# Other slots for the third and fourth batches' stages beside the shared FFN

## The chip, the cores and the metric

The kernel runs on one core of a Trainium2 chip. The metric is the device time in microseconds (us) of one execution. Three runs of the kernel before gave 1532.86, 1532.9 and 1529.8 us; their median is 1532.86 us. A change of under 0.2%, about 3 us, can hardly be told from none.

The engines have short names in the profile: PE is TensorE (PEld its weight loads), DVE is VectorE, ACT is ScalarE, POOL is GpSimd and SP is SyncE, which only issues DMAs here. Each engine runs its own instructions in order, and waits on semaphores for the others.

## The reference

Four batches of 512 tokens with 512 features go through one pre-norm decoder layer:

```
x = x + attention(layernorm(x))        # 32 heads of 64, 8 key/value heads, rotary, causal
x = x + xattn(layernorm(x), ctx)       # einsum('emk,enk->emn', xq, wq), see below
x = x + ffn(layernorm(x))              # shared FFN on all tokens + 8 experts, top 1, 256 slots each

xq = quant_dequant_act_1x128(x)        # amax of each 128 features, scaled to 448, rounded to fp8, scaled back
wq = quant_dequant_weight_128x128(ctx) # the same with one amax for each 128x128 block
flat = where(pos < C, eidx * C + pos, E * C)   # pos: how many earlier tokens chose this expert
shared = silu(xt @ sw1) * (xt @ sw3) @ sw2     # 704 hidden features
```

So for each batch, between attention and FFN: normalise, find the peak of each group of 128, scale, round, turn (transpose), multiply with the turned and rounded context, add, normalise again, turn again, and compute the eight router logits, the choice, and each token's place in its expert.

## The kernel before, in words

All matrix products are in fp32 made of split operands: a high part (`h`) and a low part (`l`), and three matmuls for each product (`three`, L514 to L516). So every turned tile is copied out of PSUM twice: ACT writes the high part (`turn`, L1007), and then DVE subtracts it from the bank and writes the low part (`turn_lo`, L1392).

The program is one long order written out by hand for each engine. Attention takes the first 1035 us or so. Then the shared FFN goes over the tokens in eight half batches `x` = 0 to 7 (256 tokens each), then come the eight experts. Each `x` has eight steps `k`: `k` = 0 to 4 are up-projections of 24 matmuls (128x256), `k` = 5 is one of 12, `k` = 6 is the down-projection (30 matmuls of 128x512) and `k` = 7 is its last 4 matmuls, after which DVE adds the result to X (L1544). With every up-projection ACT computes the silu out of PSUM (L1054) and a high part (L1041), and DVE the product (`hm`, L1529) and a low part (`Hl`, L1516).

Beside the FFN of batch b-1 run the stages between attention and FFN of batch b; its router stages run beside its own FFN. `slots()` gives each stage of each batch a slot number, and before step `k` of half batch `x` every engine calls `side_slot(8 * x + k - 5)`, which issues that engine's part of the stages with that number. So slot 7 stands before x1 k4, slot 11 before x2 k0, slot 16 before x2 k5, slot 19 before x3 k0; for batch b (2 and 3, the third and the fourth) slots are counted from s = 16(b-1), 16 or 32. The stages are

- `stats2`, `norm2`: DVE, mean and variance of X, and the inverse root (L1185 to L1196, then L1373);
- `look`: ACT, the normalised tile into `T1` or `T2` (L945); `peaks`: DVE, its group maxima (L1378); `scales`: DVE (L1314 to L1319);
- `scaled`: ACT, four instructions on a tile (L971); `cross_round`: DVE two instructions (L1328, L1330), then POOL an addition, a subtraction and a scaling (L1744, L1746, L1748);
- `context_turn`, `cross_turn`, `route_turn`: PE turns a tile with four transposes (L506), ACT and DVE copy it out. SP loads a later tile when a context tile has been turned;
- `cross_product`: 12 matmuls of 128x512 into bank 6, then DVE adds the bank to X (L1397); `stats3`, `rstd3`, `norm3`: DVE (L1204, L1185 to L1196, L1209);
- `logits`: 12 matmuls into bank 6, ACT copies them (L1015); `choose`: PE turns them, DVE works in 12 small instructions (L1422 to L1441); `place`: two small matmuls into bank 6 (L700, L701), then 8 small DVE instructions (L1450 to L1462); `scatter`: POOL, four indirect DMAs (L1790).

Three rules of the order matter below.

1. Turned tiles of this stretch use two banks, 0 and 1, in turn: PE begins the turn number q when both ACT's and DVE's copies of turn number q-2 are done (`turn`, the wait on `others[q - 2]`). The order of the turns is that of the slots; inside one slot `place(x)` sorts context turns first, then route turns, then cross turns.
2. In DVE's `side_slot` all other stages of a slot go first; the copies `turn_lo` and the additions `cross_add` come last (`ends`). Only then come DVE's parts of the FFN step.
3. Bank 6 is shared by cross products, logits, `choose` and `place`; each waits until DVE or ACT has taken the previous one out (`wait_bank6`).

Of the kernel before, what the change touches and what calls it, by code (L numbers as in the profile page):

```python
# [5 lines left out]
NT, D, NB, TB = 16, 512, 4, 4  # L6
# [29 lines left out]
def slots():  # L36

    side = {}


    def plan(s, stage, b, i=0):
        side.setdefault(s, []).append((stage, b, i))

    first = ("route_turn", "cross_turn", "logits", "choose", "place", "cross_product")
    for i in range(TB):
        plan(-36 + i, "context_turn", 0, i)
        plan(-32 + 2 * i, "cross_turn", 0, i)
        plan(-31 + 2 * i, "cross_product", 0, i)
        plan(-30 + 2 * i, "stats3", 0, i)
        plan(-22 + i, "norm3", 0, i)  # L50
        plan(-20 + i, "route_turn", 0, i)
        plan(-16 + i, "context_turn", 1, i)
    plan(-23, "rstd3", 0)
    plan(-6, "logits", 0)
    plan(-4, "choose", 0)
    plan(-2, "place", 0)
    plan(3, "scatter", 0)
    for i in range(TB):
        plan(-44 + 2 * i, "stats2", 1, i)
        plan(-14 + i, "look", 1, i)  # L60
        plan(-12 + i, "peaks", 1, i)
        at = (-4, -3, -1, 1)[i]
        plan(at - 1, "scaled", 1, i)
        plan(at, "cross_round", 1, i)
        plan((-1, 0, 1, 3)[i], "cross_turn", 1, i)
        plan((0, 1, 2, 4)[i], "cross_product", 1, i)
        plan((1, 2, 3, 5)[i], "stats3", 1, i)
        plan(7 + i // 2, "norm3", 1, i)
        plan(9 + i // 2, "route_turn", 1, i)
    plan(-36, "first_root", 1)  # L70
    for i in range(3):
        plan(-34 + 2 * i, "root", 1, i)
    plan(-28, "bias", 1)
    plan(-8, "scales", 1)
    plan(6, "rstd3", 1)
    plan(12, "logits", 1)
    plan(14, "choose", 1)
    plan(19, "place", 1)
    plan(19, "scatter", 1)
    for b in range(2, NB):  # L80
        s = 16 * (b - 1)
        for i in range(TB):
            plan(s - 13 + i, "stats2", b, i)
            plan(s - 4 + i + i // 3, "context_turn", b, i)

            late = i // 3
            plan(s - 8 + i, "look", b, i)
            plan(s - 7 + i, "peaks", b, i)
            plan(s - 3 + i + late, "scaled", b, i)
            plan(s - 2 + i + late, "cross_round", b, i)  # L90
            plan(s + i + late, "cross_turn", b, i)
            plan(s + 1 + i + late, "cross_product", b, i)
            plan(s + 2 + i + late, "stats3", b, i)
            plan(s + 7 + i // 2, "norm3", b, i)
            plan(s + 9 + i // 2, "route_turn", b, i)
        plan(s - 9, "norm2", b)
        plan(s - 4, "scales", b)
        plan(s + 6, "rstd3", b)
        plan(s + 12, "logits", b)
        plan(s + 14, "choose", b)  # L100
        plan(s + (19 if b < NB - 1 else 15), "place", b)
        plan(s + (19 if b < NB - 1 else 15), "scatter", b)
    for i in range(2):
        plan(16 * NB - 13 + i, "load_x", i)
        plan(16 * NB - 9 + i, "expert_turn", 0, i)
    plan(16 * NB - 11, "load_slots", 0)

    def place(x):
        return first.index(x[0]) if x[0] in first else len(first) - 9 * (x[0] == "context_turn")

    for s in side:
        side[s].sort(key=place)
    return side
# [12 lines left out]
def decoder(nc, x_in, ctx_in, wqkv_in, wo_in, wg_in, wf_in, ident_in, mask_in, rope_in, ksin_in, rank_in, tri_in, out):  # L126
# [3 lines left out]
    with ExitStack() as root:  # L130
# [146 lines left out]


        side = slots()
        in_order = [x for s in sorted(side) for x in side[s]]  # L280
        turns = [x for x in in_order if x[0] in ("context_turn", "cross_turn", "route_turn", "expert_turn")]
# [1947 lines left out]
```

## Time and profile before

| | us |
|---|---|
| median of three runs | 1532.86 |
| profiled execution, its own time | 1531.05 |
| its span, first to last instruction | 1529.0 |
| PE busy | 1436.9 (94%) |
| DVE busy | 1150.9 (75%) |
| POOL busy | 1029.5 (67%) |
| ACT busy | 984.4 (64%) |

The span is cut by the profile in 40 slices. PE is busy in nearly all of them to nine tenths or more; the slices 27 and 28 (about 1032 to 1108 us), where the shared FFN begins, show 8. The mean granted TensorE clock of the execution is 0.990 of full speed. A wait is told in the profile as idle time of an engine and what ended it; "issue" is idle time for which the profile found no releaser.

### The profile page before, as it was taken

Reading aid. Unit: us, or ns where it says so; the run is one execution under the profiler, and the core shown is the slowest. Engines: PE = TensorE matmul, PEld = TensorE weight load, DVE = VectorE, ACT = ScalarE, POOL = GpSimd, SP = SyncE. Lnnn points to the kernel's source line nnn. Section 1 sums busy time; section 2 is a strip of 40 time slices with the busy share of each in tenths; the row PEclk is TensorE's granted clock in tenths of the full one; section 3 lists DMA queues with packets and bytes.
Section 4 is the critical chain, followed back from the end, with each engine's and each line's share of the span. In section 5 each row is a group of like instructions: output and inputs, shape, how many; then the busy total and the mean of one; then the engine's idle time right before and its main releaser. Section 6 shows DMA issues by size and latency. Waiting matters only on the chain.

```text
span 1529.0 us, 26946 instructions
## 1 busy us (share of the span) xinstructions
PE 1436.9 (94%) x8617; PEld 1257.7 (82%) x8617; DVE 1150.9 (75%) x2810; ACT 984.4 (64%) x2510; POOL 1029.5 (67%) x1057
## 2 busy tenths in 40 slices
PE   5899999999999999999999999888899999999997
PEld 3778888888878888778888887777787888999996
DVE  7678888887887787887888788788675753677773
ACT  4687786777777887778878787756241412555562
POOL 3787888888877788888898888754313131366663
PEclk9999999999999999999999999999999999999999
DMA  6445454334322424334244342503111011587772
GB/s 211 120 118 171 123 142 133 87 113 124 83 81 62 115 74 128 89 82 121 69 119 124 80 128 60 172 13 130 58 42 43 21 42 39 172 266 239 250 245 81
DMA packets 108620, 174.74 MB, mean 114 GB/s; under 512 B 20936, under 2 KB 42696, under 8 KB 108480
## 3 DMA queue, kind: packets, MB, share of 16 engines
q1 hardware_dynamic: 104448, 160.51, 35.9%
q0 software_dynamic: 3840, 12.25, 2.2%
q8 instruction: 70, 1.15, 0.3%
q14 instruction: 70, 0.57, 0.1%
q10 hardware_dynamic: 192, 0.26, 0.1%
HBM read 94.05 MB, written 33.18 MB: 83 GB/s over the span
## 4 chain that ended last, share of the span: by engine, by line
PE 67%; DVE 12%; ACT 12%; issue 5%; DMA 2%; POOL 1%; SPq 1%; DVEq 0%; POOLq 0%; ACTq 0%
PE bank L514 15%; PE bank L516 15%; PE bank L515 15%; PE bank L566 5%; ACT P L914 5%; PE bank L532 4%; PE bank L581 4%; PE bank L582 3%; PE bank L533 3%; DVE P L1261 2%; ACT PTh L926 2%; DVE PTl L1302 2%; PE bank L506 2%; ACT Otmp L920 2%; DVE Opair L1296 1%
## 5 line engine op out<-in xcount | busy, mean ns | idle before, releaser
L914 ACT ACTIVATE P<-P,mn 128x512 f32<-128x512 f32 (+3 forms) x512 | 284.6, 557 | 211.4 <-DVE mn L1261 207.5
L1701 POOL TENSOR_TENSOR P<-P,ri 128x128 f32<-128x128 f32 (+3 forms) x512 | 360.1, 734 | 31.1 <-DVE ri L1250 31.0
L1261 DVE CUSTOM_DVE_ANT_0 P<-bank,mask 128x512 f32<-128x512 f32 (+3 forms) x512 | 236.6, 480 | 83.8 <-PE bank L533 82.3
L1302 DVE TENSOR_TENSOR PTl<-bank,PTh 128x512 fp32r<-128x512 f32 (+1 forms) x384 | 229.6, 599 | 33.5 <-ACT PTh L926 30.6
L566 PE MATMUL bank<-ident,P 128*128 128x128 f32 x1280 | 201.6, 272 | 2.5 <-POOL P L1701 2.5
L926 ACT ACTIVATE PTh<-bank 128x512 fp32r<-128x512 f32 (+1 forms) x384 | 197.7, 516 | 3.4 <-PE bank L566 0.5
L532 PE MATMUL bank<-KT,QT 128*128 128x256 f32 (+2 forms) x512 | 188.3, 368 | 7.4 <-DVE mn L1261 7.4
L581 PE MATMUL bank<-PTh,VS 128*128 128x256 f32 (+2 forms) x512 | 161.3, 326 | 10.9 <-DVE X L1311 4.3
L514 PE MATMUL bank<-XT,Wh 128*128 128x512 f32 x384 | 163.6, 426 | 7.7 <-DVE XT L1232 3.5
L533 PE MATMUL bank<-KT,QT 128*128 128x256 f32 (+2 forms) x512 | 166.0, 324 | 0.0
L582 PE MATMUL bank<-PTl,VS 128*128 128x256 f32 (+2 forms) x512 | 154.5, 324 | 0.0
L516 PE MATMUL bank<-XT,Wl 128*128 128x512 f32 x384 | 152.8, 398 | 0.0
L515 PE MATMUL bank<-XT,Wh 128*128 128x512 f32 x384 | 152.4, 397 | 0.0
L566 PEld LDWEIGHTS bank<-ident,P 128*128 128x128 f32 x1280 | 149.3, 141 | 3.0 <-POOL P L1701 3.0
L1739 POOL TENSOR_TENSOR OTl<-Opair,OTh 128x512 fp32r<-128x512 f32 x64 | 83.4, 1303 | 90.0 <-ACT OTh L1001 89.2
L514 PE MATMUL bank<-Oh,OTh 128*128 128x512 f32 x256 | 105.7, 413 | 18.0 <-DVE Opair L1296 15.5
L581 PEld LDWEIGHTS bank<-PTh,VS 128*128 128x128 f32 x512 | 96.2, 188 | 25.8 <-issue 13.2
L1296 DVE TENSOR_TENSOR Opair<-bank,Otmp 64x512 f32<-64x512 f32 x128 | 87.3, 682 | 38.3 <-ACT Otmp L920 37.1
L532 PEld LDWEIGHTS bank<-KT,QT 128*128 128x128 f32 x512 | 96.8, 189 | 22.7 <-DVE mn L1261 10.5
L1054 ACT ACTIVATE hm<-bank 128x256 f32<-128x256 f32 x96 | 36.3, 378 | 111.7 <-PE bank L516 111.0
L533 PEld LDWEIGHTS bank<-KT,QT 128*128 128x128 f32 x512 | 97.6, 191 | 10.4
L582 PEld LDWEIGHTS bank<-PTl,VS 128*128 128x128 f32 x512 | 96.2, 188 | 9.9
(229 smaller groups left out, 4097.7 us busy)
## 6 DMA issues: line engine op xcount, KB each, us to landing
RW<-in_wf SPq DMA_DIRECT2D x153, 256.0 KB, 3.5
QT<-qh SPq DMA_DIRECT2D x256, 64.0 KB, 2.0
QT<-ql SPq DMA_DIRECT2D x252, 64.0 KB, 2.0
Oraw<-in_wo SPq DMA_DIRECT2D x16, 512.0 KB, 4.9
KT<-KT SPq DMA_DIRECT2D x32, 256.0 KB, 3.0
Wraw<-in_wqkv SPq DMA_DIRECT2D x9, 768.0 KB, 4.9
xnx<-in_ctx SPq DMA_DIRECT2D x24, 256.0 KB, 3.6
saved<-Wh SPq DMA_DIRECT2D x7, 768.0 KB, 3.5
```

The lines of the kernel that those rows point to most:

```text
L514: e.matmul(ps, lh, rh, start=start, stop=False)
L515: e.matmul(ps, lh, rl, start=False, stop=False)
L516: return e.matmul(ps, ll, rh, start=False, stop=stop)
L532: e.matmul(ps[:, 0:k], lhs, KT[:, u % 2, 0, 0:k], start=True, stop=False)
L533: e.matmul(ps[:, 0:k], lhs, KT[:, u % 2, 1, 0:k], start=False, stop=True).then_inc(p_s, 1)
L566: last = e.transpose(ps[:, tokens(m)], src, ident[:, :])
L581: e.matmul(ps[:, q:512], lhs, pt_of(PTh, kb), start=kb == 0, stop=False)
L582: last = e.matmul(ps[:, q:512], lhs, pt_of(PTl, kb), start=False, stop=kb == 3)
L914: e.activation(pq, pq, ACT.Exp, bias=mn[:, z, qb:qb + 1], scale=-1.0, accum_out=rs[:, z, qb:qb + 1]).then_inc(a_exp, 1)
L1261: e.tensor_tensor_reduce(P[:, z, off[qb]:off[qb] + k], bank[n % 2][:, 0:k], mask[:, 512 - k:512], -0.125, BIG, ALU.add, ALU.min, mn[:, z, ...
L1302: e.tensor_tensor(pt_part(PTl, part), bank[2 + part][:, 0:128 * n].rearrange("p (m n) -> p m n", n=128), pt_part(PTh, part).bitcast(F32), ...
L1701: e.tensor_tensor(pq, pq, ri[:, z, qb:qb + 1].to_broadcast([128, n]), ALU.mult).then_inc(g_norm, 1)
```

## The change

Only `slots()` changes, and in it the slots of stages of batches 1 to 3. No instruction is added or removed; the order of the instructions on the engines changes.

```
-    plan(12, "logits", 1)
-    plan(14, "choose", 1)
-    plan(19, "place", 1)
+    plan(11, "logits", 1)
+    plan(12, "choose", 1)
+    plan(15, "place", 1)
     plan(19, "scatter", 1)
     for b in range(2, NB):
         s = 16 * (b - 1)
         for i in range(TB):
             plan(s - 13 + i, "stats2", b, i)
-            plan(s - 4 + i + i // 3, "context_turn", b, i)
+            plan(s - 9 + i, "context_turn", b, i)
 
             late = i // 3
-            plan(s - 8 + i, "look", b, i)
-            plan(s - 7 + i, "peaks", b, i)
-            plan(s - 3 + i + late, "scaled", b, i)
-            plan(s - 2 + i + late, "cross_round", b, i)
+            plan(s - 8 + i // 2, "look", b, i)
+            plan(s - 7 + i // 2, "peaks", b, i)
+            at = s + (-3, -2, 0, 2)[i]
+            plan(at - 1, "scaled", b, i)
+            plan(at, "cross_round", b, i)
             plan(s + i + late, "cross_turn", b, i)
             plan(s + 1 + i + late, "cross_product", b, i)
             plan(s + 2 + i + late, "stats3", b, i)
             plan(s + 7 + i // 2, "norm3", b, i)
             plan(s + 9 + i // 2, "route_turn", b, i)
         plan(s - 9, "norm2", b)
-        plan(s - 4, "scales", b)
+        plan(s - 5, "scales", b)
         plan(s + 6, "rstd3", b)
-        plan(s + 12, "logits", b)
-        plan(s + 14, "choose", b)
-        plan(s + (19 if b < NB - 1 else 15), "place", b)
-        plan(s + (19 if b < NB - 1 else 15), "scatter", b)
+        plan(s + 11, "logits", b)
+        plan(s + 12, "choose", b)
+        plan(s + (15 if b < NB - 1 else 14), "place", b)
+        plan(s + (19 if b < NB - 1 else 14), "scatter", b)
```

For batch 2 this gives the slots that follow (batch 3's are 16 more; the routing stages named are batch 1's, those of batch 2 are 16 more).

```
slot  step    before                                            after
 7    x1 k4   norm3 1.0 1.1, norm2                              the same, context turn 0
 8    x1 k5   norm3 1.2 1.3, look 0                             the same, look 1, context turn 1
 9    x1 k6   route turns 1.0 1.1, peaks 0, look 1              context turn 2, route turns 1.0 1.1, peaks 0 1, look 2 3
10    x1 k7   route turns 1.2 1.3, peaks 1, look 2              context turn 3, route turns 1.2 1.3, peaks 2 3
11    x2 k0   peaks 2, look 3                                   logits 1, scales
12    x2 k1   context turn 0, logits 1, peaks 3, scales         choose 1, scaled 0
13    x2 k2   context turn 1, scaled 0                          round 0, scaled 1
14    x2 k3   context turn 2, choose 1, round 0, scaled 1       round 1
15    x2 k4   round 1, scaled 2                                 place 1, scaled 2
16    x2 k5   context turn 3, cross turn 0, round 2             cross turn 0, round 2
17    x2 k6   cross turn 1, product 0, scaled 3                 the same
18    x2 k7   cross turn 2, product 1, round 3                  the same
19    x3 k0   place 1, product 2, scatter 1                     product 2, scatter 1
```

## Rows read from the trace of the kernel before

**Rows 1.** The page: busy us by engine; the silu's group (busy us, mean ns | idle).
```profile
PE 1436.9 (94%) x8617; PEld 1257.7 (82%) x8617; DVE 1150.9 (75%) x2810; ACT 984.4 (64%) x2510; POOL 1029.5 (67%) x1057
...
L1054 ACT ACTIVATE hm<-bank 128x256 f32<-128x256 f32 x96 | 36.3, 378 | 111.7 <-PE bank L516 111.0
```

**Rows 2.** PE's waits, 1200 to 1274 us: us in total, times, longest.
```profile
PE bank L506 <- POOL work L1748: 3.6, 2, 2.3
```

**Rows 3.** PE in order of time at batch 2's cross turns: start, us, idle before.
```profile
1145.27 0.63 PE L506 MATMUL bank<-ident,work 128*128 128x128 f32 x4 [1.22 <-POOL work L1748]
...
1149.62 0.63 PE L506 MATMUL bank<-ident,work 128*128 128x128 f32 x4 [2.28 <-POOL work L1748]
1150.01 0.58 PE L514 MATMUL bank<-XT 128*128 128x512 f32 x1
...
1154.20 0.40 PE L516 MATMUL bank<-XT 128*128 128x512 f32 x1
...
1166.87 0.47 PE L514 MATMUL bank<-XT 128*128 128x512 f32 x1 [1.16 <-DVE lp L1451]
```

**Rows 4.** Stretches: length, PE busy, granted clock, DMA share, GB/s.
```profile
1063.00:1070.00 7.00, 4.78 (x39) 1.00 0.14 51
...
1149.00:1154.00 5.00, 4.38 (x15) 0.66 0.00 0
```

**Rows 5.** PE in order of time, x1 k4 (from 1109.85) to x2 k0.
```profile
1109.85 0.28 PE L514 MATMUL bank<-XT,Uh 128*128 128x256 f32 x1
...
1114.07 1.04 PE L506 MATMUL bank<-ident,XN 128*128 128x128 f32 x8
...
1121.80 1.03 PE L506 MATMUL bank<-ident,XN 128*128 128x128 f32 x8
...
1124.45 0.36 PE L514 MATMUL bank<-YT,Uh 128*128 128x256 f32 x1 [0.69 <-issue]
```

**Rows 6.** DVE in order of time, same stretch.
```profile
1114.59 0.16 DVE L1373 SCALAR_TENSOR_TENSOR ssum<-mv,rstd 128x4 f32<-128x4 f32 x1
1114.67 0.42 DVE L1516 TENSOR_TENSOR Hl<-hm,Hh 128x256 fp32r<-128x256 f32 x1
...
1115.33 1.00 DVE L1209 TENSOR_SCALAR XN<-X,mv,rstd 128x512 f32<-128x512 f32 x2
...
1117.04 0.68 DVE L1378 TENSOR_REDUCE aam<-work 128x4 f32<-128x512 f32 x1
1117.74 1.29 DVE L1392 TENSOR_TENSOR YT<-bank,YT 128x512 fp32r<-128x512 f32 x2
...
1123.06 1.29 DVE L1392 TENSOR_TENSOR YT<-bank,YT 128x512 fp32r<-128x512 f32 x2 [2.86 <-ACT YT L1007]
```

**Rows 7.** Batch 3: the end of its norm2 on DVE, the route turns on PE.
```profile
1190.10 0.16 DVE L1373 SCALAR_TENSOR_TENSOR ssum<-mv,rstd 128x4 f32<-128x4 f32 x1
...
1188.80 1.04 PE L506 MATMUL bank<-ident,XN 128*128 128x128 f32 x8
```

**Rows 8.** POOL and DVE at batch 2's roundings.
```profile
1145.49 1.40 POOL L1744 TENSOR_TENSOR work<-work 128x512 f32<-128x512 f32 x1 [0.36 <-DVE work L1330]
...
1148.38 1.10 POOL L1748 TENSOR_TENSOR work<-work,asc 128x512 f32<-128x512 f32 x1
...
1140.25 0.42 DVE L1328 TENSOR_SCALAR work<-work 128x512 uint32<-128x512 uint32 x1
...
1147.21 1.37 DVE L1330 TENSOR_SCALAR work<-work 128x512 f32<-128x512 f32 x1
```

**Rows 9.** DVE's place: batch 1's (first two), then batch 0's.
```profile
1166.46 0.16 DVE L1450 COPY cum<-cum 128x8 bf16<-128x8 bf16 x1
...
1167.64 0.17 DVE L1462 CAST sidx<-sm 128x4 uint32<-128x4 f32 x1
...
1069.54 1.23 DVE L1450 COPY cum<-cum 128x8 bf16<-128x8 bf16 x1
...
1073.34 0.17 DVE L1462 CAST sidx<-sm 128x4 uint32<-128x4 f32 x1
```

## The prediction

> **What bounds the kernel now.** I read the page first: PE is busy for 1436.9 of 1529.0 us [rows 1], so time can be won only where PE idles, and every new wait of PE is lost time. Then PE's waits by stretch. From 1200 to 1274 us, which is batch 3's stages, PE waits 3.6 us in two goes for POOL's last rounding instruction [rows 2]; batch 2, 75 us earlier, shows the two single waits, and one for DVE's `place` [rows 3], which batch 3 repeats with the same 1.16. The reader is to see three things there: 1.22 and 2.28 us before cross turns 0 and 1, 1.16 us before product 2, and, behind the 2.28, a product at half pace. Its 12 matmuls run from 1150.01 to about 1154.43, 4.4 us, where the full pace of 0.23 to 0.24 us gives 2.8: 1.6 us more. The granted clock in that stretch is 0.66 of 2.4 GHz, so for most of it 1.2 GHz, and what came before was PE idle twice [rows 4].
>
> Last I read DVE and PE side by side where the change puts the context turns, slots 7 to 10. PE is never idle there until the 0.69 before x2 k0 [rows 5], which I read as the wait for DVE's copy of the last route turn: it starts at 1123.06 and two take 1.29, 1124.35 [rows 6]. DVE though is behind: when PE begins its route turns at 1114.07, DVE has just ended batch 2's norm2 (1114.59), a stage of slot 7, two slots back [rows 5, 6].
>
> **What goes.** (a) Rounding. Tile 0 is rounded in slot 13 and tile 1 in slot 14, and their cross turns stay in 16 and 17. POOL needs 4.0 us a tile (1145.49 to 1148.38 + 1.10) [rows 8]. Between slots 13 and 16 lie three up-projections of 2.8 us (24 matmuls; 1109.85 to 1114.07 is 36 of them, 0.117 each) [rows 5]. I count from the start of the logits (0): they take 2.8, k0 ends at 5.6, `choose` takes 0.4 of PE, k1 ends at 8.9, k2 at 11.7. Silu and product end some 0.9 behind a step (an estimate: ACT's 0.38 [rows 1] and as much for DVE), so DVE rounds tile 0 from 9.8 to 10.7, POOL is done at 14.6, and PE asks at 17.4. DVE's two instructions for tile 1 begin at 12.6 and end behind POOL's second and third, at 14.9; POOL is done at 19.0, PE asks at 19.25, after k5 of 1.4. Both waits go: 3.5 + 3.6 = 7.1 us. (b) With them the slow product: 2 x 1.6 = 3.2. (c) `place` stands four slots earlier, where no product follows at once: 2 x 1.2 = 2.4. Sum 12.7 us.
>
> **What moves at no cost.** Logits and `choose` are as long as before, and k0 (2.8 us) still lies between them for ACT's copy. The context loads that SP issues behind each context turn come 20 us before their use. The scatter can start as soon as POOL has rounded tile 3; batch 3's stages 43 to 46 have four FFN steps until the first expert loads. Should one of them be late it would be an idle row of PE at x7 k4; I take 0, at most 1 us either way.
>
> **What comes: three turns in one slot on two banks.** In slot 9 PE now has context turn 2, route turn 0, route turn 1, and each waits for DVE's copy of the turn two before. DVE makes those copies last in its slot, and it is behind. In steps, for batch 2, with DVE unchanged up to 1114.67 [rows 6]:
> - copy of context turn 0: a copy takes 0.69, the next begins 0.6 on: to 1115.27;
> - the FFN's two instructions, 0.66 (1114.67 to 1115.33): 1115.93;
> - norm3 of two tiles, 1.0: 1116.9; copy of context turn 1, done 1117.6, DVE free 1117.5;
> - FFN's two: 1118.2; peaks 0 and 1, 0.7 each (1117.04 to 1117.74), both in slot 9 now: 1119.6;
> - copy of context turn 2, done 1120.3.
>
> PE is there at 1114.07 + 2 x 0.44 = 1114.95 (four transposes take 0.44; two context turns stand before it). It may make route turn 1 only at 1120.3, with two turns of 0.44 done meanwhile: 5.35 - 0.9 = 4.5 us idle. Those turns themselves only moved. For batch 3 norm2 ends 1.30 us after PE's 1188.80, not 0.52 [rows 7], so 0.8 more: 5.2 (4.46 + 0.78).
>
> The down-projection starts behind a stretch with more idle time than that of rows 3, so I take one fall of the clock per batch at the price that one had: 2 x 1.6 = 3.2. Bounds: 0 (a wait of PE of 2.05 us in 1063 to 1070 left the clock at 1.00 [rows 4]) and two falls, 6.4.
>
> Slot 10 again has three turns; DVE is level by then, as PE has had 7 us of down-projection. From the start of two turns to the end of DVE's first copy it takes 1121.80 to 1123.06 + 0.69, 1.95 us [rows 5, 6], during which PE makes one turn besides the first (0.88): 1.1 us idle, for both batches 2.3. The 0.69 after k7 stays.
>
> **What comes in slots 15 to 17.** `place` now meets POOL rounding tile 1. Its DVE chain takes 1.3 us with POOL idle (batch 1, 1166.46 to 1167.8) and 4.0 with POOL at work (batch 0, 1069.54 to 1073.5) [rows 9]; DVE's rounding instruction goes from 0.42 to 1.37 in the same way [rows 8]. I take 3.9, since the neighbour is the same; on the count above DVE then goes through place (15.5 to 19.4, behind k3's product), two FFN instructions, round 2 (0.9) and the copy of cross turn 0 (to 21.5), while PE wants product 0 at 19.7: 1.9 us idle. With the short chain it is 0.8. Two batches: 3.8, bounds 1.6 and 7.0 (with a fall of the clock each).
> By the Trainium skill (SBUF — State Buffer, "Who interferes with whom") a DVE copy, cast or tensor_scalar in a two-port mode and a GpSimd instruction shut each other out for a whole instruction. By it a chain with a copy and several tensor_scalars is the long one, 3.9, and not the 1.3 that batch 1's own rows show with POOL idle; on this the trace agrees, by batch 0's 4.0 us, and the sum would be 2.2 us lower by the other.
>
> **Sum.** 4.5 + 5.2 + 3.2 + 2.3 + 3.8 = 19.0 come, 12.7 go: +6.3 us. The profiled execution took 1531.05, 1.8 us under the median of the runs, 1532.86; it would come to 1537.4, and the median to 1539.2.
>
> **Rivals.**
> - *DVE is not the queue (faster).* The one point that decides is whether DVE is over 1 us behind PE at the end of k5. If it keeps level, each third turn costs what it costs in slot 10: 4 x 1.15 = 4.6, no fall, and products wait 2 x 0.8: 6.2 against 12.7, -6.5 us, 1526.4. For it: DVE is only 75% busy [rows 1], and 2.86 us idle just after. Against it: the row of norm2 at 1114.59, in a slot that PE had left 2 us before. Chance 0.13.
> - *The waits come, the clock stays, `place` is short.* 4.5 + 5.2 + 2.3 + 1.6 = 13.6 against 12.7: +0.9, 1533.8. For it: the 1.00 of 1063 to 1070. Chance 0.16.
> - *The rounding is still awaited.* Tile 1 has a margin of 0.25 us only. If POOL's three instructions are held up by DVE's as the latter are by them, cross turn 1 waits up to the old 2.3 us and product 0 behind it runs slowly: +3.2, 1542.4. Chance 0.08.
> - *The clock falls behind the small waits too* (slot 10 and product 0), four times 1.6: 1545.6. Chance 0.10.
>
> The forecast itself has 0.53. Slower by over 0.2% (3 us; less is not told from no change) are the forecast and the last two, 0.71; within are the second's, 0.16; faster 0.13. The range for 8 in 10 runs from 1531 to 1546: it takes in the second rival and the last, and leaves out the first. The forecast's own is 1536 to 1543.
>
> **What would show it.** Right: PE's waits in slot 9 and 10 of batches 2 and 3 before L506, released by DVE's L1392 (or shown as "issue"), some 4.5, 5.2 and twice 1.1 us, and a granted clock under 1 in the down-projection behind; no wait on L1748 but batch 1's; no wait on L1451 but none before a product. A wait of 1 to 2 us before product 0, with L1392 or ACT's copy as its end. Wrong: no idle time of PE between x1 k5 and x1 k7, or a DVE that copies context turn 2 before 1118 us; or place's instructions at 0.2 us each beside POOL. Then the first rival holds.

## The result and the profile after

The changed kernel takes 1538.47 us (median of six runs, 1536.21 to 1540.1) against 1532.66 us before in the runs beside it: 1.0044 of the time, 95% interval 1.0032 to 1.0056. So it is slower, by 5 to 9 us, and the forecast was 1539.2. Its profiled execution took 1536.21 us with a span of 1534.1, 5.1 over the span of before.

Line numbers are one higher than before, since `slots()` has one line more (e2 and e4 below keep the old ones). The page first: PE busy (us, share, instructions) hardly differs [rows 1].

```profile
PE 1440.2 (94%) x8617; PEld 1260.4 (82%) x8617; DVE 1150.9 (75%) x2810; ACT 984.7 (64%) x2510; POOL 1029.2 (67%) x1057
```

PE in order of time, the rows before which it sat idle (start, busy, instruction, in brackets the idle time and what ended it by the profile), and where batch 2's down-projection begins and ends (1121.01, 1129.06). These answer to [rows 3] and [rows 5]:

```profile
1115.39 0.63 PE L507 MATMUL bank<-ident,work 128*128 128x128 f32 x4 [0.36 <-issue]
1117.57 0.63 PE L507 MATMUL bank<-ident,XN 128*128 128x128 f32 x4 [1.55 <-ACT XT L1008]
1120.27 1.09 PE L507 MATMUL bank<-ident,XN 128*128 128x128 f32 x4 [2.07 <-issue]
1121.01 0.78 PE L515 MATMUL bank<-Dh,Hh 128*128 128x512 f32 x1
...
1129.06 0.60 PE L507 MATMUL bank<-ident,work 128*128 128x128 f32 x4
...
1131.12 0.63 PE L507 MATMUL bank<-ident,XN 128*128 128x128 f32 x4 [1.02 <-ACT YT L1008]
...
1133.21 0.47 PE L515 MATMUL bank<-YT,Gh 128*128 128x512 f32 x1 [0.53 <-issue]
...
1154.95 0.47 PE L515 MATMUL bank<-XT 128*128 128x512 f32 x1 [1.43 <-ACT XT L1008]
...
1192.99 0.63 PE L507 MATMUL bank<-ident,work 128*128 128x128 f32 x4 [1.15 <-issue]
1195.17 1.09 PE L507 MATMUL bank<-ident,XN 128*128 128x128 f32 x4 [1.55 <-ACT XT L1008]
1197.87 1.09 PE L507 MATMUL bank<-ident,XN 128*128 128x128 f32 x4 [1.61 <-ACT XT L1008]
...
1209.14 0.63 PE L507 MATMUL bank<-ident,XN 128*128 128x128 f32 x4 [1.02 <-ACT XT L1008]
...
1232.86 0.47 PE L515 MATMUL bank<-XT,YT 128*128 128x512 f32 x1 [1.50 <-ACT YT L1008]
```

The reader is to see three turns in slot 9, each with a wait before it: 0.36, 1.55 and 2.07 us for batch 2 (4.0), 1.15, 1.55 and 1.61 for batch 3 (4.3); one wait of 1.02 in slot 10; 1.43 and 1.50 before product 0. No row of batches 2 and 3 names POOL or `place` any more.

DVE in the same stretch, which answers to [rows 6]:

```profile
1114.61 0.69 DVE L1393 TENSOR_TENSOR XT<-bank,XT 128x512 fp32r<-128x512 f32 x1
...
1115.87 1.00 DVE L1210 TENSOR_SCALAR XN<-X,mv,rstd 128x512 f32<-128x512 f32 x2
1116.78 0.69 DVE L1393 TENSOR_TENSOR XT<-bank,XT 128x512 fp32r<-128x512 f32 x1
...
1118.18 1.27 DVE L1379 TENSOR_REDUCE aam<-work 128x4 f32<-128x512 f32 x2
1119.47 0.69 DVE L1393 TENSOR_TENSOR XT<-bank,XT 128x512 fp32r<-128x512 f32 x1
```

Each L1393 here is the copy of a context turn. They end at 1115.30, 1117.47 and 1120.16; PE's three turns start at 1115.39, 1117.57 and 1120.27, each 0.1 behind. The profile names ACT or nothing at all as what ended the waits; by the times it was DVE.

The granted clock by stretch (length, PE busy, clock, DMA share, GB/s), against [rows 4]:

```profile
1114.00:1120.20 6.20, 2.29 (x17) 0.98 0.25 85
1120.20:1124.00 3.80, 3.73 (x12) 0.58 0.02 4
1195.00:1202.00 7.00, 5.22 (x16) 0.51 0.00 0
1149.00:1155.00 6.00, 4.57 (x40) 1.00 0.00 0
```

The beginnings of both down-projections run at 1.2 GHz for the most part. The last stretch holds batch 2's two cross turns and the wait behind them and is at 2.4 GHz; product 0, behind it, takes 2.8 us (1154.95 to 1157.79), where it took 4.4 before.

### The profile page after: what moved, and what is told of

Read it like the earlier page. It is cut to its first block, busy times and chain, and to the rows that moved or that the text cites. A ratio compares the mean times of both kernels' runs of the same rounds, so it can differ in the third digit from the quotient of the medians.

```text
span 1534.1 us, 26940 instructions
## 1 busy us (share of the span) xinstructions
PE 1440.2 (94%) x8617; PEld 1260.4 (82%) x8617; DVE 1150.9 (75%) x2810; ACT 984.7 (64%) x2510; POOL 1029.2 (67%) x1057
## 3 DMA queue, kind: packets, MB, share of 16 engines
q8 instruction: 70, 1.15, 0.3%
## 4 chain that ended last, share of the span: by engine, by line
PE 65%; ACT 13%; DVE 13%; issue 5%; DMA 2%; POOL 1%; SPq 1%; DVEq 0%; POOLq 0%; ACTq 0%
PE bank L515 15%; PE bank L517 14%; PE bank L516 14%; PE bank L567 5%; ACT P L915 5%; PE bank L582 4%; PE bank L533 4%; PE bank L583 4%; PE bank L534 3%; DVE P L1262 2%; ACT PTh L927 2%; DVE PTl L1303 2%; ACT Otmp L921 2%; PE bank L507 2%; DVE Opair L1297 1%
## 5 line engine op out<-in xcount | busy, mean ns | idle before, releaser
L927 ACT ACTIVATE PTh<-bank 128x512 fp32r<-128x512 f32 (+1 forms) x384 | 197.8, 516 | 3.9 <-PE bank L567 1.0
L515 PE MATMUL bank<-Oh,OTh 128*128 128x512 f32 x256 | 106.4, 416 | 17.9 <-DVE Opair L1297 14.9
L533 PEld LDWEIGHTS bank<-KT,QT 128*128 128x128 f32 x512 | 96.7, 189 | 21.6 <-DVE mn L1262 9.4
```

The costliest lines, as they stand in the source:

```text
L515: e.matmul(ps, lh, rh, start=start, stop=False)
L533: e.matmul(ps[:, 0:k], lhs, KT[:, u % 2, 0, 0:k], start=True, stop=False)
```

## The experiments

The attention part and the first slots, which the change doesn't touch, differ by some 6 us between profiled executions (the cross turn of batch 1 that PE waits 2 us for starts at 1064.74 in one and at 1070.97 in another). So beside the medians I use the *stage*: from the start of that turn to the start of x6 k0 (its logits, where they stand in front of it). It is 207.2 us before (1066.35 to 1273.57) and 213.1 in the changed kernel (1065.79 to 1278.87), 5.9 more. Part of such a difference is chance. From that turn to batch 1's cross turn 2 all kernels but e10 and e11 run the same program, and yet this takes 14.9 us in one profiled execution and 16.3 in another, as the clock falls at one point or another. The last column begins at cross turn 2 and leaves this out: 192.3 before (from 1081.27) and 197.7 in the changed kernel (from 1081.20), 5.4 more. Each is one execution.

| kernel | median, us | ratio to before (95%) | stage, us | from cross turn 2, us |
|---|---|---|---|---|
| before | 1532.66 | | 207.2 | 192.3 |
| changed | 1538.47 | 1.0044 (1.0032 to 1.0056) | 213.1 | 197.7 |
| e1 context turns back | 1521.38 | 0.9936 (0.9922 to 0.9950) | 197.8 | 181.6 |
| e2 context turns only | 1547.80 | 1.0101 (1.0086 to 1.0117) | 222.2 | 207.0 |
| e3 rounding only | 1525.90 | 0.9957 (0.9944 to 0.9971) | 200.7 | 185.3 |
| e4 router only | 1527.40 | 0.9964 (0.9951 to 0.9978) | 205.2 | 188.9 |
| e5 context turns in 7, 8, 11, 12 | 1525.11 | 0.9953 (0.9941 to 0.9965) | 201.6 | 186.7 |
| e6 place back | 1537.4 (one run) | | 212.9 | 197.8 |
| e8 copies first | 1537.32 (one run) | | 211.1 | 194.9 |
| e9 context turns in 12 to 15 | 1522.25 | 0.9930 (0.9917 to 0.9942) | 196.8 | 181.6 |
| e10 e9, batch 0's place later | 1519.77 | 0.9920 (0.9906 to 0.9933) | 195.2 | 182.9 |
| e11 e10, all places later | 1519.84 | 0.9920 (0.9907 to 0.9933) | 195.0 | 182.8 |

The ratios are to runs of the kernel before made beside each kernel, whose median was 1531.4 to 1532.9 us.

**e1: context turns back.**

```
-            plan(s - 9 + i, "context_turn", b, i)
+            plan(s - 4 + i + i // 3, "context_turn", b, i)
```

> The changed kernel with the context turns of batches 2 and 3 back in their old slots (12, 13, 14, 16), all else as changed. Theory (three turns in a slot on two banks, behind a late DVE): the waits of slots 9 and 10 go (4.0 + 1.0 and 4.3 + 1.0 us in the changed kernel's trace) with the slow clock behind them (some 5 us), the rounding's and place's gains stay; four copies of 0.6 us come back to DVE beside the rounding, so product 0 waits about 2 us instead of 1.45. 1524 to 1526 us, faster than both. Rival (the new rounding order and place beside POOL are what costs): no wait goes that matters, 1535 or more.

1521.38 us: 17 us under the changed kernel and 0.64% under before. PE's idle rows from batch 1's logits (slot 11) to the end of the stage are these, and no others but the 0.69 before each logits:

```profile
1124.12 0.47 PE L515 MATMUL bank<-YT,Gh 128*128 128x512 f32 x1 [0.69 <-issue]
...
1146.53 0.63 PE L507 MATMUL bank<-ident,work 128*128 128x128 f32 x4 [0.80 <-issue]
...
1215.97 0.63 PE L507 MATMUL bank<-ident,work 128*128 128x128 f32 x4 [0.90 <-issue]
```

The theory holds and the rival falls. The size was off to the good side, by 3 us against the expected 1524 to 1526: I expected 2 us before product 0, and there is none; in its place stand 0.8 and 0.9 before cross turn 1.

**e2: context turns only.** The same line the other way round, in the kernel before.

> The kernel before with only the context turns moved to slots 7 to 10. Theory: PE waits about 3.5 and 4 us in slot 9 (one group maximum less in DVE's queue than in the changed kernel) and 1.0 in slot 10, the clock falls behind them, and the old waits for POOL (3.5 us a batch) and for place (1.2) stay: 12 to 14 us over before, 1545 to 1546. Rival: about the time of before, 1533.

1547.80 us, 1.01% over before, 2 us more than expected. Slot 9 of batch 2:

```profile
1117.92 0.63 PE L506 MATMUL bank<-ident,work 128*128 128x128 f32 x4 [0.36 <-issue]
1120.10 0.63 PE L506 MATMUL bank<-ident,XN 128*128 128x128 f32 x4 [1.55 <-ACT XT L1007]
1122.20 1.04 PE L506 MATMUL bank<-ident,XN 128*128 128x128 f32 x4 [1.48 <-ACT YT L1007]
```

The third wait is 1.48, not 2.07: one group maximum (0.6 us of DVE) less stands before the copy that it needs. This is the harmful part of the change by itself, some 15 us.

**e3: rounding only.**

```
-            plan(s - 8 + i, "look", b, i)
-            plan(s - 7 + i, "peaks", b, i)
-            plan(s - 3 + i + late, "scaled", b, i)
-            plan(s - 2 + i + late, "cross_round", b, i)
+            plan(s - 8 + i // 2, "look", b, i)
+            plan(s - 7 + i // 2, "peaks", b, i)
+            at = s + (-3, -2, 0, 2)[i]
+            plan(at - 1, "scaled", b, i)
+            plan(at, "cross_round", b, i)
...
-        plan(s - 4, "scales", b)
+        plan(s - 5, "scales", b)
```

> The kernel before with only look, peaks, scales, scaled and cross_round of batches 2 and 3 moved as in the change. Theory: the two waits for POOL (3.5 and 3.6 us) and the slow products behind them (3.2) go, a wait of about 1.4 us a batch before product 0 comes: 7 us under before, about 1525.5. Rival (uneven rounding is what makes the change slow): 1533 or more.

1525.90 us, as expected. PE's waits from 1110 to 1300 us (us in total, times, longest):

```profile
PE bank L507 <- DVE XT L1393: 3.0, 2, 1.6
PE bank L515 <- DVE lp L1452: 2.3, 2, 1.2
PE bank L515 <- issue: 2.1, 3, 0.7
```

POOL is gone from the list. The residual 1.4 and 1.6 us stand before cross turn 1, where PE waits for DVE's copy of context turn 3, the turn two before, and not before product 0 as I had expected.

**e4: router only.** Only the lines of logits, choose, place and batch 3's scatter, as in the change.

> The kernel before with only logits, choose and place (and batch 3's scatter) moved as in the change. Theory: the 1.2 us before product 2 goes in both batches; choose no longer stands before round 0 on DVE, so tile 0's rounding is done in time (1.2 us a batch), while place beside POOL (3 to 4 us instead of 1.3) holds round 1 back, so cross turn 1 still waits some 2 us: 4 to 5 us under before, about 1528. Rival (place beside POOL costs more than it gives): slower than before, 1534 or more.

1527.40 us, as expected. Its profiled execution was its slowest run (1532.41); the last column is 3.4 us under before, with the clock down behind both waits. These are:

```profile
1153.62 1.09 PE L506 MATMUL bank<-ident,work 128*128 128x128 f32 x4 [2.69 <-POOL work L1748]
...
1225.91 1.09 PE L506 MATMUL bank<-ident,work 128*128 128x128 f32 x4 [2.75 <-POOL work L1748]
```

Cross turn 0 and product 2 wait no longer, cross turn 1 waits 2.7 for the rounding (2 were expected): `place`'s chain (1146.40 to 1148.6, 2.2 us where 3 to 4 were expected) now stands on DVE before its part of that rounding. The rival falls: place beside POOL costs less than it gives, though barely (by e6 below 0.9 against 1.17 us a batch).

The parts add up nearly. By their ratios e3 and e4 are -6.6 and -5.5 us, together -12, and e1, which has both, is at -10, within the intervals. With e2's +15.5 the three parts come to +3.4 us, and the changed kernel is at +6.7; that is 3 us off, which the intervals of three ratios allow. In the last column the three come to +4.3 and the changed kernel to +5.4.

**e5: context turns never with two route turns.**

```
-            plan(s - 9 + i, "context_turn", b, i)
+            plan(s + (-9, -8, -5, -4)[i], "context_turn", b, i)
```

> The changed kernel with the context turns in slots 7, 8, 11 and 12: the first two as early as in the change, but never a context turn together with two route turns. If three turns in a slot are the cost: the 1.0 us of slot 10 goes in both batches, and in slot 9 PE waits only for the copies of context turns 0 and 1, 0.4 + 1.7 us in batch 2 and some 2.9 in batch 3 instead of 4.0 and 4.3, and less of the slow clock comes: 1529 to 1531. If moving any context turn ahead of DVE's late copies costs the same: 1537 or more.

1525.11 us, better than expected. Waits of the third kind are gone in both batches:

```profile
1114.72 0.63 PE L507 MATMUL bank<-ident,XN 128*128 128x128 f32 x4 [0.35 <-issue]
1116.90 0.63 PE L507 MATMUL bank<-ident,XN 128*128 128x128 f32 x4 [1.55 <-ACT YT L1008]
...
1187.02 0.63 PE L507 MATMUL bank<-ident,XN 128*128 128x128 f32 x4 [1.16 <-issue]
1189.20 0.63 PE L507 MATMUL bank<-ident,XN 128*128 128x128 f32 x4 [1.55 <-ACT XT L1008]
```

and with these 1.9 and 2.7 us of idle time the clock of the stretches 1110 to 1125 and 1180 to 1200 us is 1.00. So of the 13 us by which it beats the changed kernel (11 in the last column), the third turns and the clock behind them are most. What is left of the early context turns is the waits for the copies that DVE is late with: e5 is still 3.7 us slower than e1 by the medians.

**e6: place back in slot 19**, in the changed kernel.

> The changed kernel with place back in slot 19. If place beside POOL is what holds DVE before product 0: PE's wait before product 0 falls from 1.45 to about 0.7 us, place's eight instructions take 1.3 us again instead of 3.8, and the 1.2 us before product 2 is back; waits of slots 9 and 10 unchanged; the time within 1 us of the changed kernel's. If the wait before product 0 is the rounding's own, it stays at 1.4.

PE's waits at product 0 and product 2:

```profile
1154.87 0.47 PE L515 MATMUL bank<-XT 128*128 128x512 f32 x1 [0.49 <-issue]
...
1170.13 0.47 PE L515 MATMUL bank<-XT 128*128 128x512 f32 x1 [1.17 <-DVE lp L1452]
...
1232.80 0.47 PE L515 MATMUL bank<-XT,YT 128*128 128x512 f32 x1 [0.60 <-issue]
```

1.43 and 1.50 fall to 0.49 and 0.60, 1.17 is back: place beside POOL was about 0.9 us of each wait. The chain itself in the changed kernel and in e6:

```profile
1148.98 0.92 DVE L1451 COPY cum<-cum 128x8 bf16<-128x8 bf16 x1
...
1150.26 1.02 DVE L1456 TENSOR_SCALAR kp<-sm 128x4 f32<-128x4 f32 x1
...
1151.37 1.02 DVE L1459 TENSOR_SCALAR sm<-sm 128x4 f32<-128x4 f32 x1
...
1152.62 0.17 DVE L1463 CAST sidx<-sm 128x4 uint32<-128x4 f32 x1
```

```profile
1169.72 0.16 DVE L1451 COPY cum<-cum 128x8 bf16<-128x8 bf16 x1
...
1170.90 0.17 DVE L1463 CAST sidx<-sm 128x4 uint32<-128x4 f32 x1
```

3.8 us against 1.35, and it is the copy (eight columns) and the two tensor_scalar (four columns) that grow, from 0.17 to about 1. The last column is the same as the changed kernel's (197.8 and 197.7), so the move of place by itself is worth next to nothing.

**e8: DVE copies context turns at the head of its slot.**

```
-                    elif stage == "expert_turn":
+                    elif stage == "expert_turn" or (stage == "context_turn" and b >= 2):
                         turn_lo(x)
```

> The changed kernel, but DVE copies the context turns of batches 2 and 3 at the head of its slot, ahead of norm3, norm2 and peaks, and not behind them. If DVE's queue sets the waits of slot 9: the three of batch 2 (0.36, 1.55, 2.07 us) become about 0, 1.3 and 1.8, those of slot 10 stay at 1.0, and the time falls by 2 to 4 us. If ACT's copy sets them, as the profile's names say, nothing changes.

```profile
1120.49 0.63 PE L507 MATMUL bank<-ident,XN 128*128 128x128 f32 x4 [1.18 <-issue]
1122.91 0.63 PE L507 MATMUL bank<-ident,XN 128*128 128x128 f32 x4 [1.80 <-ACT YT L1008]
```

The first wait is gone, the others are 1.18 and 1.80 (1.96 and 1.79 in batch 3), where 1.3 and 1.8 were expected; slot 10 keeps its 1.02. ACT's program is the same, so the name ACT in those rows is not the cause. The last column is 2.8 us shorter than the changed kernel's. Part of that is the clock: behind the 3.0 us of waits in batch 2 it stayed at full speed (1.00 from 1119 to 1127 us), behind the 3.75 in batch 3 it fell. The time of one run alone tells nothing.

**e9: the fourth context turn in slot 15** (`plan(s - 4 + i, "context_turn", b, i)`).

> The kernel of e1 with the fourth context turn a slot earlier, in 15 instead of 16, away from cross turn 0. If e1's last wait (0.80 and 0.90 us before cross turn 1) is for DVE's copy of context turn 3, the turn two before: it goes, and the time falls by 1 to 2 us under e1, to about 1520. If it is for the rounding on POOL, it stays.

1522.25 us, no different from e1. The waits before cross turn 1 go, so they were for the copy of context turn 3; but 0.94 and 1.03 us come before product 0 instead. DVE is late there, and which copy PE meets first depends on the order. So moving the turn only moves the wait along PE's queue. What DVE is late by is `place`: e11 below, which moves it away, has no wait before product 0.

**e10 and e11: batch 0's place, then all places, between later products.**

```
-    plan(-2, "place", 0)
+    plan(3, "place", 0)
```

> The kernel of e9 (the change with context turns in 12 to 15) with batch 0's place moved from slot -2, where it meets POOL's roundings, to slot 3, between two products. If place beside POOL holds DVE (3.9 us in batch 0's rows), the 3.0 us before batch 1's product 0 goes and part of the slow clock with it: 3 to 5 us under e9, about 1518. If that wait is the rounding's own, nothing goes: 1522.

> The kernel of e10 with place and scatter of batches 1 and 2 in slots 20 and 36, behind the last rounding and between products 2 and 3, where nothing waits for bank 6 at once. The 0.94 and 1.03 us before product 0 in e9 go or fall under 0.3, no wait comes at product 3: 1.5 to 2 us under e10, about 1516.5. Rival: the scatter, one slot later, is late for norm3 (slot 23), DVE waits for it and PE with it: 1519 or more.

1519.77 us for e10, 2.5 us under e9's median, less than the 3 to 5 expected, and the intervals overlap. The 3.03 before batch 1's product 0 halves to 1.61 and that product runs at full clock; to cross turn 2 it takes 12.3 us where e9 takes 15.1. But a new wait appears before product 3:

```profile
1067.76 1.09 PE L507 MATMUL bank<-ident,work 128*128 128x128 f32 x4 [2.71 <-POOL work L1749]
...
1075.71 0.47 PE L515 MATMUL bank<-XT,YT 128*128 128x512 f32 x1 [1.61 <-ACT YT L1008]
...
1098.50 0.47 PE L515 MATMUL bank<-XT,YT 128*128 128x512 f32 x1 [1.12 <-issue]
```

The place chain of 1.3 us stands before the copy of cross turn 3 in DVE's queue, and that copy (from 1097.74) is what product 3 needs. e11 does the same to batch 2: 0.98 us before product 3 at 1173.97 in place of 0.92 before product 0; batch 3's is 0.21. Its expected 1.5 us more did not come, 1519.84; nor did the rival's late scatter: PE has no idle row there. So place in its later slots too delays a copy that PE waits for, by about 1 us, only 0.21 in batch 3. Both are 0.8% under before and 1.2% under the changed kernel by the medians, the best versions run here.

## Why the prediction was right

The sign, the size (forecast +6.3 us, medians +5.8, the last column +5.4) and the places of the waits were right. The steps, one by one:

- *Three turns, two banks, slot 9.* Forecast 4.5 us idle in batch 2, 4.0 found. From PE's arrival to its third turn it is 5.24 us where 5.35 was counted: DVE's norm3 took 0.91 and not 1.0, its two group maxima 1.27 and not 1.4. Batch 3: forecast 5.2, found 4.3 idle, and 6.03 us from arrival to third turn where 6.1 was counted. e2 shows the cost by itself, e8 that it is DVE's order, e5 that it is the third turn.
- *Slot 10.* Found 1.02, of which 0.16 comes back in the wait after k7 (0.53, 0.69 before), so 1.7 in both batches. The forecast put down 2.3, but its own working gives 1.07 for one and 2.1 for two.
- *The clock.* Forecast two falls at 1.6 us. The down-projections last 8.05 us (1121.01 to 1129.06) and 8.5 (1198.61 to 1207.08), where before 6.94 stood [rows 5, with the 0.79 of its turns]: 1.1 and 1.5.
- *What goes.* 12.7 us: no wait on L1749 or L1452 is left in batches 2 and 3, and the products run at full clock.
- *Product 0.* Forecast 1.9, found 1.43 and 1.50. The long place chain (forecast 3.9, found 3.8) was the right one to take, and DVE's queue came out as counted: its copy of cross turn 0 ends 21.6 us behind the start of the logits, 21.5 in the forecast. It was PE that came later: cross turn 1 starts at 19.7 where 19.25 was counted, as 24 matmuls took 2.87 us there and not 2.8.
- *Not in the sum: what the turns themselves hold PE.* Before, slot 9 and slot 10 each held PE for two turns in a row, 0.79 us, and the lone context turn for 0.36. With waits between them the three turns of slot 9 hold it for 2.0 us in batch 2 and, with two of them at the slow clock, 2.5 in batch 3, those of slot 10 for 1.4 each. Over the four slots that is 2.7 us more than before.

Sum of what was found: 8.3 + 1.7 + 2.6 + 2.7 + 2.9 - 12.7 = +5.5 us, where the last column shows 5.4. The four terms that the forecast had came to 15.5 us, not 19.0, and the 2.7 us of the turns, which it did not have, made up for most of that. So the mechanism was right, and that the total is within a microsecond is in part luck.

The rival that would have made it faster needed DVE level with PE at the end of k5. PE was at slot 9 at 1115.03, and DVE had just ended slot 7's norm2 and still had the copy of slot 7's context turn to make (1114.61 to 1115.30). The rival on the rounding was close: tile 1's POOL work ends at 1152.37 in the changed kernel, and cross turn 1 starts without a wait at 1152.92.

## What to carry to other kernels

When stages are moved to earlier slots, count per slot what rotates through a small set of banks: the third user of two banks waits for the slowest of its two readers, and for everything that stands before that reader's copy in its queue. A slot that looks empty on the engine that bounds may be the one in which another engine is two slots behind; look there at that engine's rows, not at its busy share. Here the good part of the edit (-10 us) and the bad one (+15) were nearly independent, so taking the bad one out gave a kernel faster than both.

## What was not expected of the hardware

- Tiny DVE instructions (4 or 8 columns) of the kinds copy and tensor_scalar took about 1 us instead of 0.17 while POOL ran a tensor_tensor, and each ended with POOL's current instruction: L1451, L1456 and L1459 at 1149.90, 1151.28 and 1152.39, POOL's three at 1149.88, 1151.25 and 1152.37. The same held for a larger tensor_tensor with both inputs in SBUF (L1517, 1.41 us at 1144.36, 0.42 alone). A tensor_tensor that reads one input out of PSUM (L1530, 0.42 at 1148.65) and the small reduce (L1454, 0.19 at 1150.03) ran inside POOL's instructions at their usual length. The small scalar_tensor_tensor (L1457) fell into a gap between two of them, so nothing is shown about it.
- These runs give no limit for the idle time that brings the granted clock down. It fell behind 4.0 us of PE idle in three pieces (changed kernel, batch 2), behind 3.75 in two (e8, batch 3) and behind single waits of 2.69 and 2.75 us (e4). It stayed at 1.00 behind 1.9 and 2.7 us in two pieces (e5) and 3.0 in two (e8, batch 2). And the same wait in the same program went both ways: behind 2.05 us before batch 1's cross turn 0 the clock was at 1.00 in the kernel before [rows 4], and behind 2.08 us there it was at 0.53 for 3.5 us in e9.
